# Graph network kernel, layer 0: edge numbers read from PSUM in place of an SBUF copy, small products regrouped in their banks

## The reference

```python
h = jnp.maximum(_layernorm(x), 0.0)
summed = jax.ops.segment_sum(h[src], dst, num_segments=12500)
deg = jax.ops.segment_sum(jnp.ones(src.shape), dst, num_segments=12500)
x = x + relu(h @ W_self + (summed / max(deg, 1))[:, None] @ W_neigh + b)        # layer 0
h = jnp.maximum(_layernorm(x), 0.0)
# layer 1: per edge e = sigmoid(relu([h[src], h[dst]] @ We1 + be1) @ We2 + be2), m = e * h[src];
# sum and maximum of m over the edges of each node, then two dense products, plus x
```

## Time and profile before

| what | us |
|---|---|
| median of 3 runs (5727.77, 5729.11, 5728.72) | 5728.72 |
| span of the profiled execution | 5726.5 |
| what lies around the span, median less span | 2.2 |
| first to last one-hot instruction of layer 0 | 545.5 to 2361.0 |

### The profile page before, as it was taken

One profiled execution on the slowest core, in us unless ns is written; L12 is line 12 of the kernel. 1 busy time (PEld: TensorE's weight loads), 2 busy tenths in 40 slices (PEclk: granted clock), 3 DMA queues, 4 the chain that ended last, 5 costly groups with the idle time before them and its releaser, 6 DMA issues.

```text
span 5726.5 us, 110353 instructions
## 1 busy us (share of the span) xinstructions
PE 3700.0 (65%) x25175; PEld 3357.9 (59%) x25176; DVE 4244.9 (74%) x9019; ACT 1898.2 (33%) x4035; POOL 4144.7 (72%) x3884
## 2 busy tenths in 40 slices
PE   0001888988888888545566666666666667767771
PEld 0001878888888888545555555556555666666660
DVE  5788778877777777467777777777787778888881
ACT  6101777877777777401111111111111111111110
POOL 5243666888888888777777777777777777777766
PEclk9999999999999999855555555555555555555555
DMA  7210112434344443443333333333444434444440
GB/s 233 77 36 14 25 40 66 122 122 125 121 124 125 124 125 123 139 107 104 106 111 107 113 111 113 111 113 111 119 113 117 119 112 124 117 119 126 123 114 22
DMA packets 402218, 611.87 MB, mean 107 GB/s; under 512 B 191933, under 2 KB 274979, under 8 KB 402107
## 3 DMA queue, kind: packets, MB, share of 16 engines
q0 software_dynamic: 182688, 377.75, 24.2%
q1 hardware_dynamic: 150357, 130.12, 7.1%
q10 hardware_dynamic: 69094, 103.21, 5.9%
HBM read 470.99 MB, written 118.43 MB: 103 GB/s over the span
## 4 chain that ended last, share of the span: by engine, by line
POOL 45%; issue 21%; PE 12%; DVE 11%; DMA 3%; DVEq 2%; ACTq 2%; ACT 2%; POOLq 1%; SPq 0%; PEld 0%
POOL counts_f L572 23%; POOL extra_f L572 16%; PE ps_acc L1785 5%; POOL records L594 2%; PE ps_acc L1884 2%; DVE msg L1443 1%; POOL own_rows L618 1%; PE ps_acc L1815 1%; DMA counts_f<-hA_table,stage 1%; DVE act_w L1432 1%; PE ps L1807 1%; DVE chunk_max L1448 1%; POOL out_dram L717 1%; DVE pre L1037 1%; DVE hot L1270 1%
## 5 line engine op out<-in xcount | busy, mean ns | idle before, releaser
L572 POOL DMA_INDIRECT counts_f<-hA_table,stage x2496 | 2368.2, 949 | 783.4 <-issue 751.2
L1785 PE MATMUL ps_acc<-msg,ident 128*128 128x64 f32 (+1 forms) x4974 | 1229.8, 427 | 1013.6 <-DVE msg L1443 1013.6
L1785 PEld LDWEIGHTS ps_acc<-msg,ident 128*128 128x128 f32 x4974 | 1115.4, 328 | 1119.5 <-DVE msg L1443 1117.8
L1601 ACT ACTIVATE counts_f<-ps 128x784 bf16<-128x784 f32 x1568 | 1267.8, 823 | 427.2 <-PE ps L1807 363.8
L572 POOL DMA_INDIRECT extra_f<-hA_table,estage x780 | 1085.1, 1391 | 237.7 <-issue 232.3
L1815 PE MATMUL ps_acc<-pieces_f,counts_f 128*128 128x192 bf16 x9604 | 1035.1, 249 | 1.8 <-ACT counts_f L1601 1.2
L1807 PE MATMUL ps<-hot 128*128 128x196 bf16 x6272 | 829.8, 256 | 226.5 <-ACT counts_f L1601 153.6
L1693 ACT ACTIVATE ps<-z,be_col 128x4 f32<-128x4 f32 x854 | 228.2, 267 | 2214.4 <-DVE z L1438 1954.8
L1426 DVE TENSOR_TENSOR pre<-counts_f,ps 128x512 f32 (+1 forms) x854 | 585.4, 685 | 482.5 <-SPq L864 310.0
L1815 PEld LDWEIGHTS ps_acc<-pieces_f,counts_f 128*128 128x128 bf16 x9604 | 897.0, 139 | 3.3 <-issue 2.1
L1807 PEld LDWEIGHTS ps<-hot 128*128 128x128 bf16 x6272 | 545.0, 99 | 318.3 <-issue 292.3
(11 more groups left out here) (244 smaller groups left out, 3228.1 us busy)
## 6 DMA issues: line engine op xcount, KB each, us to landing
early_rows<-extra_f SPq DMA_DIRECT2D x196, 384.0 KB
counts_f<-early_rows ACTq DMA_DIRECT2D x98, 768.0 KB
counts_f<-hA_table,stage POOLq DMA_INDIRECT x2496
counts_f<-counts_f SPq DMA_DIRECT2D x78, 288.0 KB, 2.6
own<-own_rows ACTq DMA_DIRECT2D x98, 128.0 KB, 2.2
extra_f<-hA_table,estage POOLq DMA_INDIRECT x780
hA_table<-node ACTq DMA_DIRECT2D x98, 96.0 KB
sorted_rows<-srt SPq DMA_DIRECT2D x14, 252.0 KB, 2.6
```

The lines of the kernel that those rows point to most:

```text
L572: return pool.indirect_dma_start(to, None, table, bass.IndirectOffsetOnAxis(ap=idx, axis=axis))
L1601: act.activation(counts[:, c, nodes, :].rearrange("p (b h) t -> p b (h t)", h=2), ps_pairs[g & 1][:, :].rearrange("p (b w) -> p b w", b=BA ...
L1785: return pe.matmul(ps_sum[:, 0:D], ident[:, :], rows, start=False, stop=False, skip_group_check=True)
```

## The change

Three things.

**The numbers stay in PSUM.** `edge_transposes` writes 64 columns each for low and high numbers into `ps_val`, alone in bank `ps_t`; `hot_rows` reads `ps_val` in place of `val`. `edge_values`, its two ACT copies, the tile `val` and the semaphore `s_val` are gone. For this the rows are loaded so that partition p holds two neighbouring nodes, 2p and 2p + 1, of a pair of tiles (one DMA in place of two), so that the transpose of half of the partitions gives both parities at their place; `idx_lo` and `idx_hi` hold each number once (128 elements, before 256).

**The transposes move.** With one buffer for the numbers they can only be written when DVE has made the last one-hot rows of the tile. They go from g = 4 to the head of g = 12, behind a wait on `s_hot`; `hot_rows` of part 0 then waits on `s_tr`. `edge_ids` goes from the phases c = 0 to c = 1.

**The small products share a bank.** `h1` and `cat` transposes (`ps_T`), `product` (`ps_new`) and `ab` (`ps_ab`) all lie in `ps_y`. `cat_transpose` goes from g = 6 to g = 7, `cat_copy` from 7 to 8, `product` from 8 to 9, and the wait on `s_abs` goes from `product` to `cat_transpose`.

```diff
-        idx_lo = sb("idx_lo", [P, 2, 2, RUN], BF16)
-        idx_hi = sb("idx_hi", [P, 2, 2, RUN], BF16)
-        val = sb("val", [P, 2, 2, PAIRS], BF16)
+        idx_lo = sb("idx_lo", [P, 2 * RUN], BF16)
+        idx_hi = sb("idx_hi", [P, 2 * RUN], BF16)
...
-        ps_idx = ps_t[:, 0:P].bitcast(BF16)
+        ps_val = ps_t[:, 0:PAIRS].bitcast(BF16).rearrange("p (w n) -> p w n", w=2)
+        ps_T = ps_y[:, 0:P]
+        ps_new = ps_y[:, P:P + D]
+        ps_ab = ps_y[:, BANK // 2:BANK]
...
-                v.tensor_copy(idx_lo[:, :, :, :], twice(src_lo[:, :])).then_inc(s_prep, 1)
-                v.tensor_copy(idx_hi[:, :, :, :], twice(src_hi[:, :])).then_inc(s_prep, 1)
+                v.tensor_copy(idx_lo[:, :], src_lo[:, :]).then_inc(s_prep, 1)
+                v.tensor_copy(idx_hi[:, :], src_hi[:, :]).then_inc(s_prep, 1)
...
             def hot_rows(q, c, s):
                 if s == 0:
-                    wait_alone(v, s_val, q * 4 + (2 * c + 2))
+                    wait_alone(v, s_tr, q * 2 + (c + 1))
...
-                    ids = val[:, c, which, s * SUB_PAIRS:(s + 1) * SUB_PAIRS].rearrange("p (b e) -> p b e", e=2)
+                    ids = ps_val[:, which, s * SUB_PAIRS:(s + 1) * SUB_PAIRS].rearrange("p (b e) -> p b e", e=2)
...
-                if ids and c == 0:
+                if ids and c == 1:
                     edge_ids(q + 1)
...
-                    act.activation(val[half, k & 1, :, :], by_parity[half, :, :, h], ACT.Copy).then_inc(s_val, 1)
...
-                    if g == 4 and ids:
-                        edge_values(q, c + 1)
...
-                    if g == 7 and mean:
+                    if g == 8 and mean:
                         cat_copy(q - 1, c)
...
+                half = slice((k & 1) * PAIRS, ((k & 1) + 1) * PAIRS)
                 for w, ids in ((0, idx_lo), (1, idx_hi)):
-                    last = pe.transpose(ps_idx[:, w * P:(w + 1) * P],
-                                        ids[:, k & 1, :, :].rearrange("p h k -> p (h k)"), ident_b[:, :])
+                    last = pe.transpose(ps_val[:, w, :], ids[half, :], ident_b[half, half])
...
             def cat_transpose(q, c):
                 wait_alone(pe, s_cat, q * 4 + (2 * c + 2))
-                pe.transpose(ps_t[:, P:2 * P], cat[:, :], ident[:, :]).then_inc(s_catT, 1)
+                if not isinstance(q, int) or q * 2 + c:
+                    wait_alone(pe, s_abs, q * 4 + 2 * c)
+                pe.transpose(ps_T, cat[:, :], ident[:, :]).then_inc(s_catT, 1)
...
+                    if g == 12 and ids:
+
+                        wait_alone(pe, s_hot, q * (4 * SUBS) + (c + 1) * (2 * SUBS))
+                        edge_transposes(q, c + 1)
                     if new:
                         pairs(q, c, g)
...
-                    if g == 4 and ids:
-                        edge_transposes(q, c + 1)
-                    if g == 6 and mean:
-                        if ids:
-                            wait_alone(pe, s_val, q * 4 + (2 * c + 4))
+                    if g == 7 and mean:
                         cat_transpose(q - 1, c)
-                    if g == 8 and mean:
+                    if g == 9 and mean:
                         product(q - 1, c)
```

More of the change, by code:

```diff
@@ L425, in gnn_kernel @@
         s_xadd = sem("s_xadd")
-        s_win = [sem(f"s_win{c}") for c in range(2)]
+        s_win = sem("s_win")
         s_prep = sem("s_prep")
         s_tr = sem("s_tr")
-        s_val = sem("s_val")
         s_hot = sem("s_hot")
@@ L785, in next_tiles @@
                     wait_alone(sp, s_prep, q * 2 + 2)
-                    for c in range(2):
-                        load_edges(q * 2 + (c + 2), c)
+                    load_edges(q + 1)
                 wait_alone(sp, s_x1, q * 2 - 2)
@@ L792, in _ @@
                 sp.wait_ge(s_srtw[h], 16 * TITER)
-            for t in range(2):
-                load_edges(t, t)
+            load_edges(0)
             sp.wait_ge(s_h0w, H0_DMAS)
@@ L798, in _ @@
             sp.wait_ge(s_prep, 2)
-            for t in range(2, 4):
-                load_edges(t, t & 1)
+            load_edges(1)
             sp.wait_ge(s_prep, 4)
-            for t in range(4, 6):
-                load_edges(t, t & 1)
+            load_edges(2)
             for q in range(2, 5):
@@ L1245, in edge_ids @@
             def edge_ids(q):
-                for c in range(2):
-                    v.wait_ge(s_win[c], q * 16 + 16)
-                ids = win[:, :, :].rearrange("p c k -> p (c k)")
+                v.wait_ge(s_win, q * 16 + 16)
+                ids = win[:, :, :].rearrange("p h k -> p (h k)")
                 st.done(v.tensor_single_scalar(src_lo[:, :], ids, P - 1, ALU.bitwise_and))
@@ L1288, in new_x @@
                 wait_alone(v, s_y, q * 2 + (c + 1))
[L1289 removed]
+                v.scalar_tensor_tensor(out=node[:, c, H:H + D], in0=ps_new, scalar=0.0, in1=xh[:, c, 0:D],
                                        op0=ALU.max, op1=ALU.add).then_inc(s_x1, 1)
@@ L1606, in h1_copy @@
                 wait_alone(act, s_h1T, q * 2 + (c + 1))
-                act.activation(hT[0:D, :], ps_t[0:D, 2 * P:3 * P], ACT.Copy).then_inc(s_h1Ts, 1)
+                act.activation(hT[0:D, :], ps_T[0:D, :], ACT.Copy).then_inc(s_h1Ts, 1)
             def ab_copies(q, c):
                 wait_alone(act, s_ab, q * 2 + (c + 1))
-                act.activation(node[:, c, OWN:OWN + H], ps_y[:, BANK // 2:BANK // 2 + H], ACT.Copy).then_inc(s_abs, 1)
-                act.activation(node[:, c, 0:H], ps_y[:, BANK // 2 + H:BANK], ACT.Copy).then_inc(s_abs, 1)
+                act.activation(node[:, c, OWN:OWN + H], ps_ab[:, 0:H], ACT.Copy).then_inc(s_abs, 1)
+                act.activation(node[:, c, 0:H], ps_ab[:, H:2 * H], ACT.Copy).then_inc(s_abs, 1)
             def table_store(q, c):
@@ L1620, in cat_copy @@
                 wait_alone(act, s_catT, q * 2 + (c + 1))
-                act.activation(catT[:, :], ps_t[:, P:2 * P], ACT.Copy).then_inc(s_catTs, 1)
+                act.activation(catT[:, :], ps_T, ACT.Copy).then_inc(s_catTs, 1)
             def root(q, c):
@@ L1625, in root, with phase @@
                 act.activation(std[:, :], mv[:, 1:2], ACT.Sqrt, bias=eps_col[:, 0:1]).then_inc(s_std1, 1)
-            def phase(q, c, new=True, ids=True, mean=True, last=True):
+            def phase(q, c, new=True, mean=True, last=True):
                 for g in range(PAIR_GROUPS):
@@ L1654, in _ @@
             phase(q, 0)
[L1655 to L1658, removed]
+            phase(q, 1)
+            phase(q + 1, 0, new=False)
+            phase(q + 1, 1, new=False)
+            phase(q + 2, 0, new=False, mean=False)
             own_by_tile = own_rows.rearrange("(p t) w -> p t w", p=P)
@@ L1821, in h1_transpose @@
                 wait_alone(pe, s_h1, q * 4 + (2 * c + 2))
-                pe.transpose(ps_t[0:D, 2 * P:3 * P], node[:, c, H + D:H + 2 * D], ident[:, :]).then_inc(s_h1T, 1)
+                pe.transpose(ps_T[0:D, :], node[:, c, H + D:H + 2 * D], ident[:, :]).then_inc(s_h1T, 1)
             def ab(q, c):
                 wait_alone(pe, s_h1Ts, q * 2 + (c + 1))
-                pe.matmul(ps_y[:, BANK // 2:BANK], hT[:, :], w_ab[:, :], start=True, stop=True).then_inc(s_ab, 1)
+                pe.matmul(ps_ab, hT[:, :], w_ab[:, :], start=True, stop=True).then_inc(s_ab, 1)
             def cat_transpose(q, c):
                 wait_alone(pe, s_cat, q * 4 + (2 * c + 2))
-                pe.transpose(ps_t[:, P:2 * P], cat[:, :], ident[:, :]).then_inc(s_catT, 1)
+                if not isinstance(q, int) or q * 2 + c:
+                    wait_alone(pe, s_abs, q * 4 + 2 * c)
+                pe.transpose(ps_T, cat[:, :], ident[:, :]).then_inc(s_catT, 1)
             def product(q, c):
                 wait_alone(pe, s_catTs, q * 2 + (c + 1))
[L1834 to L1837, removed]
+                pe.matmul(ps_new, catT[:, :], w_cat[:, :], start=True, stop=False)
+                pe.matmul(ps_new, ones[0:1, 0:P], b0_row[:, :], start=False, stop=True).then_inc(s_y, 1)
             def phase(q, c, new=True, ids=True, old=True, mean=True, last=True):
```

9 lines of the change are left out of this document (3 added, 6 removed).

## The result

The changed kernel takes 5572.34 us (median of 4 runs, 5570.54 to 5573.70), the kernel before 5728.56 in the same comparison: ratio 0.9726, interval 0.9713 to 0.974. Its profiled execution took 5571.68 us with a span of 5570.0. The forecast was 5575.

What follows compares the result with a forecast made beforehand. The prediction took POOL to bound most of layer 0. Gains of 121 us in 73 phases, 17 ahead and 17 behind, less 2 for delays, gave 5575 us from 5728.7, range 5540 to 5640 (about 0.7 of the chance).

Steps and rivals of the forecast that it cites:

- POOL is the bound: Most of layer 0: POOL's gathers and scatters with issue time, 37.7 us per pair of tiles, set the other engines' pace.
- The block goes with the operand: Layer 0 gathers stand still behind one-hot instructions with two SBUF inputs; one in PSUM brings them from 1.417 to 0.95 us.
- Rival 2: The block comes with two elements per cycle, so layer 0 gathers stay held up: 5715 to 5730 us, chance 0.09.
- DVE keeps two elements per cycle from PSUM: One-hot instructions with a bf16 PSUM input stay at 0.51 ns per element; bounds no change or 1.05.
- Rival 1: One-hot instructions fall to one element per cycle with a PSUM input: about 6500 us, chance 0.13.
- ACT's copies, 0.48 per phase: Without ACT's two copies the eviction of g = 5 starts 0.48 us earlier; PE's wait at g = 8 falls to about 0.35.
- the loops of 16.85 and 16.7: Layer 0 phases after the change: PE's own loop 16.85 us, the loop through DVE part 0 and transposes 16.7; 16.9 taken.
- Rival 3: POOL is freed, but part 0 of the one-hot rows comes 0.69 us later: phases 17.4, 5610 us, chance 0.15.
- Bank and order of the small products: The transposes, copy and product move one group later; new_x comes some 0.5 us later, covered by DVE's idle 1.40 us.
- up to 0.5 in 14 phases: Cost of the later new_x in the phases with late edges, if DVE's idle time there no longer covers it.
- The sum: Gains of 121 us in 73 phases, 17 ahead and 17 behind, less 2 for delays: 5575 us.
- The 17 us ahead: Ahead of the 73 phases, POOL's 98 records scatters get 35 us shorter, 17 counted on the path; bounds 0 and 35.

Runs made afterwards that it cites:

- e6: Kernel before the change, with every second early gather of layer 0 left out (output incomplete): 5601.88 us, ratio 0.9777.
- e1: Changed kernel, but ACT copies the numbers from PSUM to SBUF once per tile at g = 12 and the one-hot instructions read that copy: 5726.75 us.
- e2: Same copy and waits as e1, but the one-hot instructions read PSUM and nothing reads the copy: 5604.65 us, ratio 0.979.
- e5: Changed kernel with the constant row of layer 1's DVE weighing instruction read from SBUF in place of PSUM: 5687.89 us, ratio 0.9927.
- e3: Changed kernel with two more ACT copies per tile at g = 4, written to a tile nothing reads: 5612.27 us, ratio 0.9794.
- e4: Changed kernel with the two transposes of the numbers at the end of g = 12, not its head: 5647.8 us, ratio 0.9859.
- f1: Changed kernel with the two transposes of the numbers between the products and sums of g = 11: 5575.04 us, ratio 0.9729.

## Why the prediction was right, point by point

**POOL is the bound.** Right: e6 takes gathers from POOL, with their DMA traffic, and the phases fall from 18.56 to 17.28; 17.34 was read off the phase shown.

**The block goes with the operand.** Right, and shown by e1 against e2. One of the three rows behind it was misread: the gather at 1115.05 starts not in the open but 0.15 us ahead of the end of the one-hot instruction that runs from 1113.97 to 1115.20, and it ends 0.82 behind that end, like the other two. It bears the same conclusion. Rival 2 (the block comes with two elements per cycle) would have needed gathers at 1.4 in the changed kernel; they are at 0.948, and e5 shows the other side.

**DVE keeps two elements per cycle from PSUM.** Right: 1.223 and 1.781 us against 1.229 and 1.784. Rival 1 fell with these rows. By them, of the two pages of the Trainium skill, section 5.1 of "Vector Engine (DVE) Microarchitecture Reference", whose conditions for two packed 16-bit values name no memory, agrees with the trace; the cap of 1x for `tensor_tensor` in "The perf-mode tier table" of "VectorE: DVE Perf Modes" doesn't.

**ACT's copies, 0.48 per phase, and the loops of 16.85 and 16.7.** Right in the sum, less so in the parts. From g = 0 to g = 8 PE needed 9.06 us before and needs 1514.53 - 1506.04 = 8.49 now, 0.57 less where 0.48 + 0.11 was forecast; from g = 8 to 12 it is 4.65, 0.1 more, as forecast; from there to the next g = 0 3.79, 0.06 more. That is 16.93 for the phase, 0.41 less than 17.34 where 0.49 was forecast. The wait at g = 8 fell by 0.35, to 0.48, and not by 0.48: PE also gets there 0.22 earlier, 0.11 by the transposes that are gone from g = 4 and 0.08 by a shorter wait for ACT at g = 2 (0.38, before 0.46). e3 measures the copies alone at 0.42 per phase, and e4 and f1 place DVE's loop just under PE's. Rival 3's wait doesn't bind, but by less than 0.1 us; for its 17.4 per phase it would have had to be some 0.5 us longer.

**Bank and order of the small products.** `new_x` now waits 35 times for PE's product, 29 us in all, and the 14 phases ahead of the first marker lost 3.0 us, as the forecast allowed ("up to 0.5 in 14 phases", 2 us taken off). No run moves these steps, or the loads and `edge_ids`, alone, so what they cost or give by themselves isn't shown.

**The sum.** Forecast against measured: 121 and 120.2 for the 73 phases, 17 less 2 for the delays and 19.0 less 3.0 ahead, 17 and 20.3 behind. In the last, from the end of DVE's last one-hot instruction to POOL's last gather of layer 0, 45 us were forecast against 62 before:

```profile
2226.17 1.78 DVE L1264 TENSOR_TENSOR hot<-ps_t,iota_hi 128x3136 bf16<-128x3136 bf16 x1
...
2273.21 0.94 POOL L573 DMA_INDIRECT extra_f<-hA_table,pieces_of  x1 [0.30 <-issue]
```

It is 45.3, 16.4 less. Of the 20.3 us behind the last marker, 15.1 lie ahead of POOL's last gather of layer 0, and 5.6 in layer 1 (from its first gather to the end 3290.1 us before, 3284.5 after; between the two 0.4 are lost). The change doesn't touch layer 1. There the 2496 gathers are 6.5 us shorter together (949 and 946 ns in the mean), and e6, which has the layer 1 of the kernel before, takes 3283.1 us with 946: so the 5.6 us seem to belong to this one profile of the kernel before and not to the change; why it is slower there stays open. The 17 us ahead, about half of a bound of 35, were close by luck: the half was a guess, and no row stood behind it.

The lower end of the range is added up wrongly: 16.7 per phase, 35 and 25 give 5535 and not 5540. Nothing hangs on it.

That the two kinds of gain overlap was in the forecast as a sequence (POOL first, then PE's new pace) and holds: 122 us for the operand (e1 less e2) and 40 for ACT's copies (e3) are 162, the change gave 156. The sum is a check of size only, since e2, with its copy at g = 12, runs at 17.29 per phase and not at 16.92. The copies were worth next to nothing while POOL set the pace, as e1 shows: it has none of the old ones at g = 4, and gains nothing.

## What to carry to other kernels

An engine that only issues indirect DMAs can be the bound without looking full: add its idle time of "issue" to its busy time, and compare the mean length of one gather between stages. If it is longer in one of them, look for DVE instructions with two SBUF inputs beside it; one operand in PSUM lifts the block, and in bf16 it cost nothing here (1.223 and 1.229 us). Then read which small instruction stands ahead of the next eviction: moving one DMA issue on ACT's queue, with two small transposes, gave 48 us, the removal of two copies 40.

## What the runs showed of the hardware that was not expected

A float instruction at one element per cycle holds POOL up just as a bf16 one does (e5: the gather ends 0.82 us behind it), and DVE shows next to no cost itself (the weighing instruction 686 ns in the mean against 681).

The block hits a gather at its start. A gather that is under way when a one-hot instruction starts keeps its length: 29 such gathers in the kernel before, 1300 to 1900 us, took 0.949 us in the mean.

On the slow chip every kernel ran a third or more slower, and the order turned: e1 took 1.017 of the time of the kernel before, e2 1.0685, e3 1.0744 and e4 1.0664, each to half a per cent. The changed kernel itself didn't run there, so whether it would be slower than the kernel before on such a chip isn't shown, but its nearest relatives are. Most single instructions kept their length (in e2 the one-hot ones 1223 and 1780 ns, the gathers of layer 0 948); it is the waits that grew. In e2 POOL's wait for ACT ahead of `own_rows` is 1399 us in all, with one of 61, where the changed kernel above has 296. Another wait in the two, in the order slow chip, then changed kernel:

```profile
POOL counts_f L575 <- PEq L1928: 872.2, 174, 17.3
```

```profile
POOL counts_f L573 <- PEq L1918: 24.5, 48, 4.7
```

PE's queue is late there, and much of the rest is "issue" or "remote", which the profile explains no further. What stalled the queues of that chip, and why the changed order suffered more from it than the old one, stays open.
